# Three 224-column matmuls into one accumulator, in place of a 448- and a 224-column one whose halves are summed

## What is computed

```python
q = (query @ wq)...            # 8 batches x 56 queries, 32 heads of 128
k = (key @ wk)...              # 8 batches x 1500 context rows, 8 heads of 128
v = (value @ wv)...            # the same
q, k = rope(q), rope(k)
raw = einsum('bhqd,bhkd->bhqk', q, k) / scale
attn = softmax(raw + mask, axis=-1)
out = einsum('bhqk,bhkd->bhqd', attn, v)
return out @ wo
```

## Time and profile before

| | us |
|---|---|
| median of three timed runs | 2133.44 (2132.41 to 2134.17) |
| the profiled execution | 2150.03 |
| its span | 2148.3 |
| mean granted TensorE clock in it | 0.977 |
| TensorE matmuls, busy | 2021.8 |
| TensorE weight loads, busy | 1791.7 |
| VectorE busy | 1279.3 |
| ScalarE busy | 1047.5 |

### The profile page before, as it was taken

How to read it: one execution, slowest core, us unless ns; L and a number is a source line. 1 busy time by engine, 2 the same in 40 slices (tenths; PEclk the granted TensorE clock), 3 DMA queues, 4 the chain that set the end, 5 groups by cost and what they waited for, 6 DMA issues and landing times. The chain is left out here.

```text
span 2148.3 us, 36505 instructions
## 1 busy us (share of the span) xinstructions
PE 2021.8 (94%) x12372; PEld 1791.7 (83%) x12372; DVE 1279.3 (60%) x2639; ACT 1047.5 (49%) x1756; POOL 312.1 (15%) x221
## 2 busy tenths in 40 slices
PE   7779999999989999899989998899999999999898
PEld 6668887889978998799978998788888998999676
DVE  7965666556655666556655666566655666666534
ACT  4444555445554555445554445455544554555522
POOL 4511111111111111111111110111111111111200
PEclk9989999999999999999999999999999999999898
DMA  5441111101121112111121112101211112111260
GB/s 189 149 154 43 14 14 51 37 14 14 14 54 42 14 14 51 43 12 14 16 53 38 14 14 55 39 14 14 40 44 23 14 14 53 33 14 14 76 223 26
DMA packets 74962, 95.00 MB, mean 44 GB/s; under 512 B 22692, under 2 KB 49444, under 8 KB 74760
## 3 DMA queue, kind: packets, MB, share of 16 engines
q1 hardware_dynamic: 74760, 92.44, 18.6%
HBM read 76.64 MB, written 15.77 MB: 43 GB/s over the span
## 5 line engine op out<-in xcount | busy, mean ns | idle before, releaser
L624 POOL TENSOR_TENSOR k_lo<-k_work,k_hi 128x500 fp32r<-128x500 f32 x192 | 244.4, 1286 | 1648.5 <-ACT k_hi L656 1648.5
L753 PE MATMUL sv_banks<-wv_hi,cT_hi 128*125 128x256 f32 x1536 | 443.7, 289 | 0.0
L753 PE MATMUL sv_banks<-wv_hi,cT_lo 128*125 128x256 f32 x1536 | 431.5, 281 | 0.0
L753 PE MATMUL sv_banks<-wv_lo,cT_hi 128*125 128x256 f32 x1536 | 431.4, 281 | 0.0
L949 DVE TENSOR_TENSOR pT<-t_banks,pT 125x448 fp32r<-125x448 f32 x384 | 236.3, 623 | 262.9 <-ACT pT L717 262.9
L717 ACT ACTIVATE pT<-t_banks 125x448 fp32r<-125x448 f32 x384 | 205.2, 543 | 346.0 <-PE t_banks L789 345.1
L924 DVE CUSTOM_DVE_ANT_0 prob<-sv_banks,mask_t 112x500 f32<-112x500 f32 x384 | 258.5, 678 | 187.3 <-PE sv_banks L777 181.4
L737 PE MATMUL k_banks<-cT_hi,wk_hi 128*128 128x500 f32 x768 | 318.7, 415 | 35.5 <-DVE k_work L862 25.7
L695 ACT ACTIVATE prob<-prob,neg_max 112x1500 f32<-112x1500 f32 x128 | 198.6, 1552 | 276.9 <-DVE neg_max L929 276.1
L737 PE MATMUL k_banks<-cT_hi,wk_lo 128*128 128x500 f32 x768 | 303.3, 395 | 0.0
L737 PE MATMUL k_banks<-cT_lo,wk_hi 128*128 128x500 f32 x768 | 303.3, 395 | 0.0
(11 more groups left out here) (125 smaller groups left out, 2987.0 us busy)
## 6 DMA issues: line engine op xcount, KB each, us to landing
stage<-in_ctx_dram SPq DMA_DIRECT2D x96, 250.0 KB
attn_by_head<-attn SPq DMA_DIRECT2D x65, 112.0 KB, 1.7
wq_raw<-in_L_xattn_wq_dram SPq DMA_DIRECT2D x7, 1024.0 KB, 6.3
q_raw<-q_by_head SPq DMA_DIRECT2D x64, 112.0 KB, 4.4
inv_b<-inv_by_head SPq DMA_DIRECT2D x64, 112.0 KB, 4.7
mask_t<-in_mask_BxSxS_ff_dram SPq DMA_DIRECT2D x16, 328.1 KB
stage<-in_L_xattn_wo_dram SPq DMA_DIRECT2D x4, 1024.0 KB, 5.5
k_work<-in_L_xattn_wo_dram SPq DMA_DIRECT2D x4, 1024.0 KB, 6.3
```

What stands on the lines that cost most here:

```text
L624: nc.gpsimd.tensor_tensor(k[1][:, c * SC:(c + 1) * SC], k_rot[:, s], f32(k[0][:, c * SC:(c + 1) * SC]), ALU.subtract).then_inc(k_lo, 1)
L753: mm = nc.tensor.matmul(sv_banks[0:ST, m % 2, t * PAIR:(t + 1) * PAIR], cT[a][:, d, tile * ST:(tile + 1) * ST], w[1][mv][:, d, g * DH:g * ...
```

## The change

For each key tile the three products become three matmuls of 224 columns, all into the left 224 columns of the bank: v_hi by the high probabilities, v_hi by the low ones, v_lo by the high ones (`PV_PASSES`). The accumulator then holds the whole sum. The copy to `o_lo`, the sum in `o_sum`, both `out` tasks and the two semaphores `o_lo_copied` and `o_free` go. `normalise` reads the bank itself, waiting for `o_ready`; with that product (`attn_ready`) the bank becomes free for the first PV of the following step. Both semaphores are given one count at the start for the step that isn't there, and the store waits for one count more.

```diff
+PV_PASSES = ((0, 0), (0, 1), (1, 0))
...
-    "even": "exp0 swap0 exp1 swap1 Q K0 T0 T1 V4 T2 swap2 T3 T4 V5 T5 K1 K2 out",
+    "even": "exp0 swap0 exp1 swap1 Q K0 T0 T1 V4 T2 swap2 T3 T4 V5 T5 K1 K2",
...
-            wait_apart(sp, attn_ready, b * HKV + (g + 1), sp_passed)
+            wait_apart(sp, attn_ready, b * HKV + (g + 2), sp_passed)
...
-                if what == "out":
-                    act.wait_ge(o_ready, b * HKV + (g + 1))
-                    nc.scalar.activation(o_lo[:, :], o_banks[:, g % 2, GQ:2 * GQ], ACT.Copy).then_inc(o_lo_copied, 1)
...
-                pe.wait_ge(o_free, b * HKV + (g + 1))
+                pe.wait_ge(attn_ready, b * HKV + (g + 1))
...
-                for a in ((1, 0) if final else (0, 1)):
-                    probs = pT[:, j % PT_SLOTS, t].rearrange("p h n -> p (h n)")[:, 0:(2 - a) * GQ]
-                    mm = nc.tensor.matmul(o_banks[:, g % 2, 0:(2 - a) * GQ],
-                                          v[a][:, 2 * j + t, (g % 2) * DH:(g % 2 + 1) * DH], probs,
-                                          start=(first and a == 0), stop=(final and a == 0), skip_group_check=True)
+                for n, (a, m) in enumerate(PV_PASSES):
+                    mm = nc.tensor.matmul(o_banks[:, g % 2, 0:GQ], v[a][:, 2 * j + t, (g % 2) * DH:(g % 2 + 1) * DH],
+                                          pT[:, j % PT_SLOTS, t, m, :], start=(first and n == 0),
+                                          stop=(final and n == len(PV_PASSES) - 1))
...
-        nc.vector.memset(o_sum[:, :], 0.0).then_inc(blank, 1)
+        dve.sem_inc(attn_ready, 1)
+        dve.sem_inc(o_ready, 1)
+        nc.vector.memset(o_banks[:, 1, 0:GQ], 0.0).then_inc(blank, 1)
...
-            dve.wait_ge(o_free, b * HKV + (RING + g))
+            dve.wait_ge(o_ready, b * HKV + (g + 1))
...
-            nc.vector.tensor_tensor(attn[:, (g - 1) % 2], o_sum[:, :], inv_b[:, :], ALU.mult).then_inc(attn_ready, 1)
+            nc.vector.tensor_tensor(attn[:, (g - 1) % 2], o_banks[:, (g - 1) % 2, 0:GQ], inv_b[:, :], ALU.mult).then_inc(attn_ready, 1)
...
-                if what == "out":
-
-                    dve.wait_ge(o_lo_copied, b * HKV + (g + 1))
-                    nc.vector.tensor_tensor(o_sum[:, :], o_banks[:, g % 2, 0:GQ], o_lo[:, :], ALU.add).then_inc(o_free, 1)
```

More of the change, by code:

```diff
@@ L522, in attention_part @@
     inv_b = sb("inv_b", [P, GQ])
-    o_lo = sb("o_lo", [P, GQ])
-    o_sum = sb("o_sum", [P, GQ])
     k_banks, sv_banks, t_banks, o_banks = ps("k_banks", RING), ps("sv_banks", RING), ps("t_banks", RING), ps("o_banks", RING)
@@ L532, in attention_part @@
     t_ready, t_hi, t_free = sem("t_ready"), sem("t_hi_ready"), sem("t_free")
-    o_ready, o_lo_copied, o_free, attn_ready = sem("o_ready"), sem("o_lo_copied"), sem("o_free"), sem("attn_ready")
+    o_ready, attn_ready = sem("o_ready"), sem("attn_ready")
     inv_stored, inv_loaded = sem("inv_stored"), sem("inv_loaded")
@@ L848, in _ @@
     def _(dve):
-        for ring in (k_free, sv_free, t_free, o_free):
+        for ring in (k_free, sv_free, t_free):
             dve.sem_inc(ring, RING)
-        nc.vector.memset(o_sum[:, :], 0.0).then_inc(blank, 1)
+        dve.sem_inc(attn_ready, 1)
+        dve.sem_inc(o_ready, 1)
+        nc.vector.memset(o_banks[:, 1, 0:GQ], 0.0).then_inc(blank, 1)
         nc.vector.memset(inv_b[:, :], 1.0).then_inc(blank, 1)
```

## The result

| | us |
|---|---|
| before, median of 7 runs | 2133.44 (2131.28 to 2136.44) |
| after, median of 7 runs | 2144.41 (2138.30 to 2148.57) |
| after by before | 1.0049, 95% interval 1.0034 to 1.0064 |
| profiled execution after | 2145.13, span 2143.4 |

The account below looks back on a forecast made before the run. TensorE's matmuls, priced start to start, were taken to bound the kernel. Splitting 768 tiles added 13.8 us, cut to 12.1 by waits hiding 8 of 64 steps, other parts zero: 2133.4 + 12.1 = 2145.5 us, range 2131 to 2155.

## What to carry over

A matmul covers its successor's weight load only if it streams long enough. So before splitting a wide moving operand to save a sum, price the pieces by the larger of columns and load, not by the sum of columns: here 448 + 224 columns cost 0.315 us and 3 x 224 cost 0.335. Work taken from engines that already wait was worth nothing here. A list of waits that leaves out the short ones can hide a wait that repeats in every other step: the idle time of a group tells. And a small transfer that a whole step waits for should not be queued behind large ones that nobody needs yet: that edit, a few lines, gave 1.3%, more than twice what the change cost, and with the matmuls of before it is the fastest kernel of this study, at 2107.7 us.

## What the runs showed of the hardware

- With 128 columns of float32r weights each, matmuls of 112 and of 224 moving columns both start 0.111 us apart; with 96 columns of weights, those of 224 start 0.103 us apart. The recorded lengths hide this: 275 ns for either width.
- Loading weights that are already loaded isn't cheaper: 274.3 and 274.2 us for PV with equal weights apart and side by side.
- After waits of 2.1 to 2.4 us, TensorE's granted clock was 0.57 to 0.61 over the next 4 us in six of seven cases in one kernel; after waits of 1.6 to 2.7 us it was 1.00 in four of seven in another. I hadn't expected the two kernels to differ in that.
- Two executions of the same kernel differed by 16 us (2150.03 and 2133.88), with 113 and 94 us of TensorE idle time between its first and its last matmul, at the same cost of all PV matmuls to 0.1 us. Of the 19 us more of idle time, 14 are in the two entries for cosine products and context tiles.
